# Cross-attention token tiles: loads moved from SyncE's queue to ScalarE's, one decoder layer on one Trainium2 core

## The reference, cut to what matters

```
x = _layernorm(x + _L0_attn_ref(x, ...))                      # gives x1
x = _layernorm(x + _L0_xattn_ref(x, ctx, ctx, bias, w_out))   # gives x2
x = _layernorm(x + _L0_ffn_ref(x, ...))

# _L0_xattn_ref: 16 heads of 32, 154 keys
logits = einsum('bhqd,bhkd->bhqk', q, k) + bias
weights = softmax(logits / sqrt(32))
attn = einsum('bhqk,bhkd->bhqd', weights, v)
return combined @ w_out
```

## Time and profile before

| | |
|---|---|
| three runs | 2289.72, 2265.87, 2286.9 us; median 2286.9 |
| profiled execution | 2284.26 us, its span 2282.5 us |
| mean granted TensorE clock | 0.955 |
| busy share of the span | PE 93%, DVE 76%, ACT 47%, POOL 36% |
| cross-attention in the span | first logits at 577 us, last quarter begins at 1269 us |

### The profile page before, as it was taken

The page is one execution under the profiler, slowest core; times in us unless marked ns, Lnnn a source line. Parts: engine busy times, 40 slices in busy tenths (PEclk is TensorE's granted clock), DMA queues, the critical chain, the costliest instruction groups (busy, mean ns, idle before and its releaser), DMA issues.

```text
span 2282.5 us, 32943 instructions
## 1 busy us (share of the span) xinstructions
PE 2111.4 (93%) x11904; PEld 1167.9 (51%) x11904; DVE 1735.8 (76%) x3296; ACT 1082.4 (47%) x1522; POOL 822.0 (36%) x802
## 2 busy tenths in 40 slices
PE   7999999984798998999999859999999699999997
PEld 3444444431586776777777524444444344444443
DVE  6768686865677897898898656777666488888885
ACT  1444444443444555555555224444444565555551
POOL 2122221222125555556455432222222134444442
PEclk9999999996779999999999779999999899999999
DMA  6334243457749969979975437888888656666662
GB/s 233 108 126 155 94 148 110 115 137 176 188 128 208 260 166 191 279 183 208 262 181 153 136 84 267 288 288 289 267 270 272 249 195 227 224 233 230 226 226 79
DMA packets 386626, 448.46 MB, mean 196 GB/s; under 512 B 279270, under 2 KB 279430, under 8 KB 368032
## 3 DMA queue, kind: packets, MB, share of 16 engines
q1 hardware_dynamic: 322448, 286.07, 46.0%
q0 software_dynamic: 64016, 160.28, 22.9%
HBM read 258.93 MB, written 138.73 MB: 174 GB/s over the span
## 4 chain that ended last, share of the span: by engine, by line
PE 82%; DVE 7%; issue 6%; ACT 1%; DMA 1%; POOL 1%; SPq 0%; DVEq 0%; POOLq 0%; ACTq 0%
PE ps_h L1708 19%; PE ps L1951 19%; PE ps_proj L600 10%; PE ps_o L1275 8%; PE ps_w L1304 7%; PE ps_s L620 5%; PE ps_m L1227 3%; PE ps_o L1271 3%; PE ps_m L1229 3%; PE ps_l L1253 3%; DVE rope_t L428 1%; PE ps_t L1289 1%; PE ps_l L1250 1%; DVE x_hi L411 1%; DVE stack L1099 1%
## 5 line engine op out<-in xcount | busy, mean ns | idle before, releaser
L1708 PE MATMUL ps_h<-xT,b_rows 128*128 128x512 f16 x2048 | 444.7, 381 | 13.1 <-DMA xT<-x_lo 13.1
L1951 PE MATMUL ps<-w,g_hi 128*128 128x512 f16 x1024 | 389.3, 380 | 21.1 <-DVE g_lo L1887 21.1
L1951 PE MATMUL ps<-w,g_lo 128*128 128x512 f16 x1024 | 389.1, 380 | 0.0
L1708 PEld LDWEIGHTS ps_h<-xT,b_rows 128*128 128x128 f16 x2048 | 200.9, 98 | 256.6 <-issue 16.6
L1549 ACT ACTIVATE h<-ps_h,b_rows 128x512 f32<-128x512 f32 x256 | 199.0, 777 | 241.5 <-PE ps_h L1708 241.5
L1275 PEld LDWEIGHTS ps_o<-vm,pT 128*128 128x128 f32 x2048 | 299.2, 202 | 13.0
L1099 DVE TENSOR_REDUCE stack<-ps_m 128x2 f16<-128x308 f32 x512 | 244.2, 479 | 55.3 <-PE ps_m L1229 53.6
L1275 PE MATMUL ps_o<-vm,pT 128*128 128x33 f32 x2048 | 284.8, 265 | 0.0
L1050 ACT ACTIVATE pT<-logit 128x512 f32<-128x512 f32 x320 | 199.0, 624 | 132.3 <-DVE logit L1117 131.4
L1622 DVE TENSOR_REDUCE amax_t<-h 128x1 f32<-128x2048 f32 x64 | 146.2, 2284 | 120.8 <-ACT h L1549 120.8
L1800 POOL TENSOR_TENSOR rstd<-vare,minus_half 128x1 f32<-128x1 f32 x64 | 152.3, 2380 | 208.5 <-DVE vare L1905 208.5
(11 more groups left out here) (182 smaller groups left out, 3840.1 us busy)
## 6 DMA issues: line engine op xcount, KB each, us to landing
hidden<-h POOLq DMA_DIRECT2D x64, 1024.0 KB, 6.7
hT<-hidden SPq DMA_DIRECT2D x64, 1024.0 KB, 6.2
xc<-x_cols SPq DMA_DIRECT2D x16, 1024.0 KB, 5.1
xr<-x_rows SPq DMA_DIRECT2D x16, 1024.0 KB, 5.5
x_rows<-x POOLq DMA_DIRECT2D x16, 1024.0 KB, 4.8
x1t<-x_rows SPq DMA_DIRECT2D x64, 256.0 KB, 3.8
bt_main<-bias_main SPq DMA_DIRECT2D x16, 1024.0 KB, 6.3
xres<-x_rows SPq DMA_DIRECT2D x64, 256.0 KB, 4.1
```

Source lines behind the costliest of these rows:

```text
L1708: mm = pe.matmul(ps_h[f % 4][:], w1[:, c, f * P:(f + 1) * P], xT[:, e, a, :, c, :], start=(a == 0 and c == 0), stop=(a == 1 and c == KC - 1))
L1951: mm = pe.matmul(ps[t][:], g[:, e, f, t * P:(t + 1) * P], w2[:, f, :], start=(f == 0 and a == 0), stop=(f == FC - 1 and a == 1))
```

## The change

In quarters with n >= 0, `load_x1` of tile q+7 leaves SP's list and becomes the first step of ACT's quarter, ahead of `copy_combined`. Its DMA goes to ACT's own queue, and its three waits (`x1_out`, `high_ready`, `low_ready`) are now ACT's. The eight quarters before q = 0 keep the load on SP. Bytes, addresses, buffers and semaphores are the same.

```
@@ SP quarter
-                if 4 * n + i >= -5:
+                if -5 <= 4 * n + i < 0:
                     load_x1(*span_at(s, b, i, 7))
@@ ACT block
+            def load_x1(s, b, t):
+                if not inside(4 * s + b, t):
+                    return
+                tile = 4 * (4 * s + b) + t
+                act.wait_ge(done.x1_out[s % 2], 16 * (2 * b + s // 2 + 1))
+                if not (isinstance(s, int) and tile < 2):
+                    act.wait_ge(high_ready, tile - 1)
+                    act.wait_ge(low_ready, tile - 1)
+                act.dma_start(x1t[:, t % 2], x1_rows[b].rearrange("(s t p) d -> s t p d", t=4, p=P)[
+                    bass.ds(s, 1), t].rearrange("s p d -> p (s d)")).then_inc(x1_in[t % 2], 16)
...
             def quarter(n, i, e):
+                if n >= 0:
+                    load_x1(*span_at(n // 4, n % 4, i, 7))
                 copy_combined(*at(n, i, -3), (e + (i - 3) // 4) % 2)
                 weights(n, i, 0)
```

## The result

Twenty executions of each kernel in turns on one chip: 2291.27 us after (median, 2280.2 to 2319.63), 2277.86 us before. The ratio is 1.0067, 95% interval [1.0043, 1.0092]: slower by about 15 us, inside the 1% that the prediction took as the least that can be told. The profiled execution took 2280.2 us, its span 2278.4 us at a mean granted clock of 0.955.

The account below looks back on a forecast made before the run. PE was taken to bound the kernel, with about 20 us of stalls to gain. 2284.3 + 16.5 (late copy) - 10 (SP relief) - 3.5 (avoided clock fall) + 7 (new falls) = 2294.3 us; own range 2275 to 2318, 8 in 10 2268 to 2342.

Parts of the forecast that it names:

- The wait in front of the copy: ACT's `combT` copy stands behind the load's wait for POOL; 16.5 us of PE time over eleven i = 2 quarters.
- No price in the other quarters: Where i is not 2, ACT's later exponentials have 1.8 us of slack, so the late copy costs nothing.
- The relief of SP: Residual loads on SP arrive 1.1 us or more sooner: 10 us gained, plus 3.5 us for one clock fall avoided.
- rival B: ACT's load issue blocks until SP's `turn_stack` issue ends, adding 31.6 us in i = 2 quarters; 2330 us, chance 0.38.
- The clock: PE idle 1.6 us in i = 2 quarters lowers its clock after 2 of 11 such waits, costing 7 us.
- the rival: In the repeat's expectation: PE waits of 1.6 us bring the clock down, some such quarter or the next lasting 15 us or more.
- The sum: Whole kernel: 2284.3 + 16.5 - 10 - 3.5 + 7 = 2294.3 us.
- The signs it named: Profile after: `combT` 1.4 us later; PE's `combT` wait 11 to 27 us; `x1t` waits under 30; DVE's unnamed about 14.
- Rivals C and D: Faster: all SP stalls and clock falls go, 2266 us; or ACT's POOL wait is never last, 2271 us; chance 0.17 together.
- H: Experiments' theory: time is lost because ACT's copy stands behind a wait for POOL; 1.36 us in each i = 2 quarter.
- R: Experiments' theory: residual tiles queued behind SP's transposes, not `x1t`, stall PE; freeing them gives ratio 0.992 to 0.999.
- O: Experiments' theory: `x1t` load in its own queue overlaps SP's transposes and slows their landing, 5.7 to 6.6 us.

Follow-up runs that it names:

- e1: Changed kernel with ACT's `x1t` load issued behind the `combT` copy instead of ahead of it; ratio 1.0052 to the kernel before.
- e3: Changed kernel with the `x1t` load behind the `combT` copy only in quarters with i = 2; ratio 1.0030 to the kernel before.
- e7: Against the kernel before: residual load at the head of ACT's quarter, `x1t` load on ACT behind the `combT` copy; ratio 0.9987.
- e6: Against the kernel before: residual load issued first in SP's quarter, nothing on ACT; 2264.35 against 2281.44 us, ratio 0.9933.
- e10: The changed kernel measured again, unaltered; ratio 1.0051 to the kernel before.
- e8: As e7, both loads on ACT, but the `x1t` load ahead of the `combT` copy; ratio 1.0054 to the kernel before.
- e2: Kernel before, loads still on SP, with only the waits for `high_ready` and `low_ready` put at the head of ACT's quarter; ratio 1.0017.
- e4: Against the kernel before: residual load moved to the head of ACT's quarter, `x1t` load staying on SP; ratio 0.9973.
- e9: e6 with the `x1t` load moved to ACT behind the copy and two exponentials, as in e5; ratio 1.0009 to the kernel before.
- e12: e6 repeated, residual load first in SP's quarter; 2265.36 against 2276.31 us, ratio 0.9946 to the kernel before.
- e11: e5 repeated, `x1t` load on ACT behind the copy and two exponentials; ratio 0.9998 to the kernel before.
- e5: Changed kernel with ACT's `x1t` load later, behind the `combT` copy and two exponentials; ratio 0.9957 to the kernel before.

## Why the prediction came out as it did

**The wait in front of the copy: right in mechanism, place and size.** Forecast 16.5 us over eleven quarters, measured 16.8 over twelve. Two details were off and cancelled: the issue takes 0.33 us (the 0.52 was SP's for the same load), so the copy starts at POOL's end + 0.53, not + 0.61; and q = 14 pays as well, since there POOL had been early only because of the stall in q = 13. e1, e3 and e7 take the wait away and bring the quarters back to 10.58 us.

**No price in the other quarters: right.** 10.37 us with the copy 1.35 us later, within the 1.8 us of slack that was counted.

**The relief of SP, 10 us and one clock fall: this step failed.** It said that a residual issued behind one load less arrives 1.1 us earlier. The issue did move: against the first logit from a median of 3.84 to 3.36 us, on average from 4.86 to 3.62. But its landing took 5.4 instead of 4.2 us (medians, 650 to 1250 us), which gives it all back. (The landing alone says little of a second queue: in e6, which has none, it took 5.5 us, and no residual was late.) e1 and e3, with the relief and without the price, have 35.5 and 32.3 us of late residuals against 28.1, and 26.8 and 32.7 us of other excess against 26.6. So the relief by itself is worth nothing. The 14.4 us of the first profile looked like the forecast gain; e10, the same kernel, has 26.8. What gain there is in the changed kernel may come another way, which the prediction named only under rival B: PE arrives later, and a tile that would have been late is then in time. That is argued, not shown. In the pair e7 and e8 the others' excess falls from 23.9 to 12.1 us as that of i = 2 rises by 16.2; one profile of each, so the size is rough.

**The clock, 7 us: not seen in the profiles.** Behind none of the twelve waits of 1.37 to 1.75 us did the clock fall within the quarter, nor behind the eleven of this kind in e10. Falls inside the counted quarters hold half speed for 17.1 us after (one fall) and 20.5 us in e10 (three), against 20.5 us before (three), so no added half-clock time shows in either profile. One thing stays open. The fall in q = 11 came 13 us after the wait of q = 10 (at 695.8 us), right behind a second PE wait of 1.83 us for a late residual at 708.2; in e10 the falls in q = 15 and 27 came in the same way, behind second waits of 1.62 and 3.40 us. By the test that e10's expectation set (the quarter or the next at 15 us or more) that speaks for the rival: q = 15 lasted 16.2 us and q = 27 17.9. Against it, q = 13 and 27 fell before behind late residuals alone (2.64 and 5.35 us). So the new wait may help a later one to bring the clock down; that wasn't tried by itself. The third fall of e10, in q = 49, came behind a wait that the profile puts down to `combT` but that ended with the late residual too:

```profile
1133.47 0.69 DVE L1158 SCALAR_TENSOR_TENSOR y<-ps_w,xres 128x512 f32<-128x512 f32 x1 [3.92 <-issue]
...
1134.31 0.59 PE L1317 MATMUL ps_w<-wo_hi,combT 128*128 128x512 f16 x2 [1.79 <-ACT combT L1078]
```

**The sum.** The ratios say 12 to 15 us slower; 16.8 us are priced, so some 2 to 5 us came back on average, at intervals of 6 or 7 us either way. The prediction had 16.5 - 13.5 + 7 = +10 us: a gain too large by about 10 us and a clock term too large by up to 7, which largely cancelled. Its nearness to the median is partly luck. It also started from one execution of 2284.3 us, 6 us above the median of twenty.

**The signs it named.** The load began 0.11 us behind POOL and the copy came 1.35 us later, as said. The wait for `combT` was to go from 11 to about 27 us: the row read there, PEld's, went to 18.9, and PE's own from 1.5 to 17.2. ACT's waits for `x1t` fell to 40.5 us (47.9 in e10), not to less than 30. DVE's unnamed waits were 13.6 us as forecast, but 26.1 in e10.

**Rival B, ACT blocked behind SP: refuted for the changed kernel.** All 57 issues took 326 to 345 ns, and 36 of them lie wholly inside the issue of one of SP's transposes. A sharp case in the profile after, q = 46:

```profile
1092.44 8.02 SPq L840 DMA_TRANSPOSE qs<-stack  x1
...
1094.80 0.33 ACTq L1029 DMA_DIRECT2D x1t<-x_rows  x1
...
1100.52 0.57 SPq L860 DMA_DIRECT2D xres<-x_rows  x1
...
1105.17 0.63 ACT L1041 ACTIVATE q<-x1t 128x512 f16<-128x512 f32 x1 [3.41 <-DMA x1t<-x_rows]
...
1105.92 0.69 DVE L1158 SCALAR_TENSOR_TENSOR y<-ps_w,xres 128x512 f32<-128x512 f32 x1 [2.11 <-issue]
```

In the midst of an issue of 8.02 us ACT's takes 0.33. The Trainium skill (Perfetto Trace Analysis, section DMA Instruction, HWDGE) has the generator locked for exclusive use, with the wait inside the issue; by it each of the 36 would have lasted until SP's issue was over, or at least until its descriptors were written, and none did. The trace contradicts it for ACT's load beside SP's transposes here, unless SP's issue holds the generator only for a small part of its time, which no row shows. One case of e7 looks like the rule, beside the smaller transpose:

```profile
923.73 1.30 ACTq L1028 DMA_DIRECT2D x1t<-x_rows  x1
...
923.85 1.23 SPq L827 DMA_TRANSPOSE q_heads<-q  x1
```

So the block that rival B feared did not come in the changed kernel, and it is rare, not unheard of, in the others. It is no free pass for the data either: the tile issued at 1094.80 was awaited until 1105.17, some 10 us later. The other rule weighed, that several issuing engines share the same 16 DMA engines (DMA: Bandwidth & Descriptors, section Issuing engines are not separate DMA queues), agrees with the landings that grew, and by it the gain would have been small, as it was. (B's own term of 31.6 us comes to about 26 us when it is added up again from POOL's ends and the issues of `turn_stack`; that would have put it nearer 2324 than 2330 us.)

**Rivals C and D: wrong.** The waits for `x1t` fell by 31.6 us without a gain, and they are as long in e6 as before without harm, so they were no part of the stalls that matter; and POOL is the last releaser of the copy in 48 quarters.

**The cause of the whole.** H is shown for the 16.8 us in the quarters with i = 2 (quarters and waits of e1, e7, e8; e2 for the wait without the load), and in the time by e8 against e7, whose intervals don't meet. For the changed kernel itself it isn't shown in the time: e1, without these 16.8 us, is as slow (1.0052), so what makes both slower than the kernel before is only in part known. R is shown for the waits by the six profiles in which the residual no longer stands behind the transposes (e4, e6, e7, e8, e9, e12): none has an unnamed wait, and all others have 13.6 us or more. For the time it is shown by e6 and e12 alone; e8 and e9 have no late residual either and are not faster than before. O has evidence in the transposes' landings: 6.4 to 6.7 us (medians) with `x1t` early on ACT's queue (after, e1, e3, e7, e8, e10), 5.9 and 6.0 with it late there (e9, e11), 5.7 to 6.0 with it on SP's. How many us of the time it costs stays open: e7 against e4 or e6 is 0.14 and 0.54%, at intervals of 0.3 to 0.4% on each. And since e9 has short landings and yet loses e6's gain, O doesn't explain e9; what does is open. It also stays open why e5 came out at 0.9957 once.

## What to carry to other kernels

A long wait on a load is a prize only if someone on the critical path waits behind it: look for the wait that reaches the bounding engine, here the residual tile that was issued behind a transpose whose issue can last 8 us, and try to reorder the queue that holds it before opening a second one. Before a load is moved to a computing engine, ask what that engine must now wait for ahead of the issue, and in which phase of the loop the next engine has no slack; the issue itself is the cheap part. And where stalls are scattered, removing one kind can bring out another (here late heads for late residuals), and two profiles of one kernel can differ by a factor of two in them, so each kernel needs its ratio beside its profile.

## What the runs showed of the hardware beyond that

- SP's issue of the residual went from a median of 433 to 573 ns, but mostly by its new place: it now stands right behind the large transpose, where `x1t`'s issue took 521 ns before, and the 54 issues that no ACT issue overlaps have a median of 572 ns. The ten that an issue of ACT overlaps took 1.28 to 1.43 us, such as the 1.43 us from 997.63 on, across ACT's issue at 998.30. That ACT's issue is the cause isn't shown: in e11 nine residual issues took 1.09 to 1.40 us with no ACT issue beside them.
- A PE wait of 1.37 to 1.75 us alone in its quarter was not followed by a lower granted clock in that quarter in any of the twelve cases after: from 726.1 us to the end of the counted quarters the clock stayed at 1.00. It is no rule for each wait of that size: before, the clock fell at 1109.5 us, about a microsecond after a PE wait of 1.47 us and in the midst of a shorter one of 0.65 us.
